# Graph layers on one core: re-timed hand-over between phases, and Z in f16 products from the twentieth tile on

## The chip, the cores and the metric

The kernel runs on 1 core of one Trainium2 chip. The metric is the device time of one execution in microseconds; lower is better. Three runs of the kernel before gave 885.96, 886.35 and 887.74, a median of 886.35 us.

## The reference, cut to what matters

```python
# x: 4096 x 256 f32, adj: 4096 x 4096 of zeros and ones
deg = max(adj.sum(-1), 1)
# layer 0: Z = x @ W0 is taken first, then the rows of adj are summed over Z
u  = adj @ (x @ W0) + x @ W0                    # pooled @ W, scaled by 1/deg
x1 = layernorm(x + relu(u / deg + x @ W0 + b0))
# layer 1
h = x1 @ Wsa;  sl = h @ a_left;  sr = h @ a_right
e = where(adj != 0, exp(-leaky_relu(sl[:, None] + sr[None, :], 0.01)), 0)
x_a = (e / (e.sum(1) + 1e-5)) @ h
x_b = adj @ (x1 @ Wg) + bg
attn_a, attn_b = sigmoid(adj @ (x1 @ wa) + x1 @ wa2 + ba), sigmoid(...)   # two gates per row
out = layernorm(x1 + sigmoid(attn_a * x_a + attn_b * x_b))
```

## The kernel before, in words

Rows are worked in tiles of 128 (T = 32), adj in strips of two row tiles by 512 columns (128 strips of 512 KB), cast to one byte ("codes") on ScalarE for even strips and on VectorE for odd ones (`cast`, L515 and L811). A ring of six strip buffers is filled by the SP queue: strip s is issued when strip s-6 is cast. Sixteen strips make one quarter (four row tiles), and the codes of each finished quarter are also written to DRAM by two DMAs of 1 MB (L324).

The order of the work on every engine is written out by hand, and engines wait on semaphores. Each engine takes its instructions in that order, so one that waits holds all behind it. The phases:

1. Z phase. For each tile t TensorE transposes x (`xt_step`, L1296), ScalarE copies it out of PSUM (`xt_copy`, L523), TensorE multiplies by W0 in f32 (`z_step`, L1307). Z is copied to SBUF by ScalarE for tiles below ZACT = 10 and by VectorE from there on (`z_copy`, L528 and L824). Z is split in two f16 parts, the high one on ScalarE (`y_hi`, L535), the low one on VectorE (`y_lo`, L851), once a scale is known that needs all of x. `split_at(t)` says how many splits stand in step t. From step 13 on TensorE adds one row block (8 matmuls, L1324) to the sums of the first four row tiles in each step. VectorE also prepares the weights of layer 1 in this phase (L858 to L875), once `load_weights` has brought them.
2. Row sums. 32 row tiles, 64 matmuls each (L1324). Two tiles behind, each tile is made into x1: VectorE `degree`, `residual`, `stats`; GpSimd the power -1/2 (L438) and a shift (L441); ScalarE `normalize` (L551); TensorE transposes x1 (`t_step`, L1344); ScalarE and VectorE split it (`x1t_copy` L560, `x1t_lo` L950); TensorE projects it by 12 matmuls (`p_step`, L1359); ScalarE `proj_copies` and VectorE `h_lo` and `forms_lo` store what layer 1 needs. The first projections stand between the quarters of tiles 4 and 5.
3. Ramp. The first products of layer 1 (`product`, L1417: seven products M1 to M7 of a Strassen step, for each pair of row tiles), the largest s over all rows (GpSimd L450), exponentials (L637), the mask on VectorE (`mask_chunk`, L1083), a high f16 part on ScalarE (`high_chunk`, L646), a low one on VectorE (`low_chunk`, L1090), and the matmuls with them (`e_chunk`, L1468, 48 matmuls).
4. Sixteen steps of layer 1 in a loop, with a tail for the last one.

In phase 3 the names below are E(s,c) for `e_chunk` of step s, chunk c; mask(s,c), high(s,c) and low(s,c) likewise.

Of the kernel before, what the change touches and what calls it, by code (L numbers as in the profile page):

```python
# [28 lines left out]
ZACT = 10  # L29
ZLAG = 12  # L30
OUTER = 16
LATE = 4
WTS = 13
WTS_AT = 8
# [54 lines left out]
def build(nc, x, adj, W0, b0, Wsa, asa, Wg, bg, Wa, ba, Wb, bb, out):  # L89
# [5 lines left out]
    class Area:  # L95
# [44 lines left out]
    wp = area("wp", [P, KD, WC], F32)  # L140
    xt = area("xt", [P, 2, D], F32)

# [36 lines left out]
    sc = area("sc", [P, 40], F32)  # L179
# [7 lines left out]
    col = iter(range(40))  # L187
# [6 lines left out]
    MH2 = column(2)  # L194

    BN, MV, VE, RS, SHIFT, DEG, REC = (
        slice(0, 6), slice(6, 8), slice(8, 9), slice(9, 10), slice(10, 11), slice(11, 12), slice(12, 13))
# [13 lines left out]
    with ExitStack() as ctx:  # L211
# [3 lines left out]
        for name in (  # L215
            "wts_in", "w0_in", "wsq_ready", "wsum_ready", "wnorm_ready", "alpha_pow",
            "const_ready", "xmax_part", "xmax_all", "wabs_ready", "wz_all", "sx_ready", "cast_act", "cast_dve",
            "xt_done", "xt_ready", "z_done", "zf_act", "zf_dve", "yhi_ready", "ylo_ready", "acc_done", "zb_ready",
            "r_ready", "stat_ready", "rstd_ready",
            "shift_ready", "x1_ready", "x1t_done", "x1t_ready", "x1t_lo_ready", "wps_ready", "proj_done",  # L220
            "g_ready", "gsum_ready", "ghi_ready", "forms_ready",
            "q_ready", "qa_ready", "hhi_ready", "hlo_ready", "nsr_ready",
            "nsr_max", "nmax_ready", "arg_ready", "rr_ready", "sl_ready", "slt_done", "slrow_ready", "sl_out",
# [184 lines left out]
        def _(pool):  # L408
# [26 lines left out]
            for n in range(T):  # L435
# [13 lines left out]
            pool.wait_ge(S["nsr_max"], 1)  # L449
            pool.partition_all_reduce(sc[:, NMAX], sc[:, NM], P, RMAX).then_inc(S["nmax_ready"], 1)  # L450
# [57 lines left out]
        def _(act):  # L508
# [9 lines left out]
            def xt_copy(t):  # L518
# [4 lines left out]
                act.copy(xt[:, t % 2, :], XTP(t)).then_inc(S["xt_ready"], 1)  # L523
# [13 lines left out]
            for t in range(T):  # L537
# [26 lines left out]
            def proj_copies(n):  # L564
# [39 lines left out]
            normalize(2)  # L604
            x1t_copy(1)
            normalize(3)
            proj_copies(1)
            x1t_copy(2)
            cast(2)
            proj_copies(2)  # L610
            x1t_copy(3)
            normalize(4)
            cast(2)
            for n in range(PT + 2, T + 3):
                proj_copies(n - 3)
                if n - 2 < T:
                    x1t_copy(n - 2)
                more = n // PT + 1 < NQ and n < T
                if more:
                    cast(1)  # L620
                if n - 1 < T:
                    normalize(n - 1)
                if more:
                    cast(1)
# [82 lines left out]
            def low_m67(u):  # L707

                gate(act, S["prod_done"], u * NPROD + NPROD, "passed_act")
# [39 lines left out]
            low_m67(0)  # L749
# [3 lines left out]
            low_m34(1)  # L753
# [33 lines left out]
            for e in range(2):  # L787
                act.wait_ge(S["attend_done"], NPAN + e)
                act.activation(sg[:, e, :], sg[:, e, :], ACT.Tanh, scale=sc[:, HINVA]).then_inc(S["sigmoid_ready"], 1)
                act.wait_ge(S["yshift_ready"], NPAN + e)  # L790
                if e == 0:
                    act.wait_ge(out_sent, 16 * (NPAN - 1))
                c, b = RS2.start + e, SH2.start + e
                act.activation(ot[:, e, :], sg[:, e, :], ACT.Identity, scale=sc1[:, c:c + 1], bias=sc1[:, b:b + 1]
                               ).then_inc(S["out_ready"], 1)
# [3 lines left out]
        def _(dve):  # L799
# [21 lines left out]
            def z_copy(t):  # L821

                dve.wait_ge(S["z_done"], t + 1)
                dve.tensor_copy(zf[:, t, 0:D], ZP(t)).then_inc(S["zf_dve"], 1)  # L824
# [9 lines left out]
            def z_scale():  # L834
# [9 lines left out]
                st.then(dve.tensor_scalar(sc[:, K64], sc[:, XG], 1.0 / EDGE_VAL, None, ALU.mult))  # L844
                dve.reciprocal(sc[:, SX], sc[:, XG]).then_inc(S["sx_ready"], 1)
# [724 lines left out]
```

## Time and profile before

| | |
|---|---|
| median of three runs | 886.35 us |
| profiled execution | 885.95 us, its span 884.1 us |
| TensorE busy | 857.5 us, 97% of the span |
| VectorE, ScalarE, GpSimd busy | 660.2, 588.4, 208.0 us |
| granted TensorE clock | 0.991 on average |
| DMA | 130.02 MB, mean 147 GB/s |

The profile is of one execution. Times in its timelines are microseconds from the start of the span, and a clock of 1.00 is full speed. An instruction's duration overlaps the next one's start by some hundredths, so prices are read from start to start.

### The profile page before, as it was taken

How to read it: one execution, taken by the hardware profiler on the slowest of the kernel's cores; microseconds unless marked ns; L12 is line 12 of the kernel's file. 1: busy time of each engine (PE TensorE's matmuls, PEld its weight loads, DVE VectorE, ACT ScalarE, POOL GpSimd, SP SyncE). 2: the span in 40 equal slices, each digit the busy share in tenths (PEclk: the TensorE clock that was granted, in tenths of full speed). 3: DMA queues.
4: the chain of work that ended last, by engine and by line, in shares of the span. 5: the costliest groups of instructions: out<-in, count | busy, mean ns of one | idle time of the engine just before them, and what ended most of it. 6: DMA issues, size and time to landing. Idle time of an engine off the chain costs nothing.

```text
span 884.1 us, 20483 instructions
## 1 busy us (share of the span) xinstructions
PE 857.5 (97%) x7573; PEld 756.1 (86%) x7573; DVE 660.2 (75%) x1146; ACT 588.4 (67%) x1246; POOL 208.0 (24%) x217
## 2 busy tenths in 40 slices
PE   7998899999999997999999999999999999999996
PEld 6887788888888885888888888888888888888886
DVE  5697465556465457898889988978978978978863
ACT  4664555655555436889877966967967867867832
POOL 1023244343433330110122022032032032032031
PEclk9999999999999999999999999999999999999999
DMA  9789999999989615101220220220220220220001
GB/s 323 226 318 328 340 352 349 382 299 347 364 299 362 217 55 193 54 8 49 79 79 1 77 77 9 68 77 0 77 77 0 77 77 0 77 77 0 25 24 37
DMA packets 67690, 130.02 MB, mean 147 GB/s; under 512 B 6544, under 2 KB 30128, under 8 KB 63152
## 3 DMA queue, kind: packets, MB, share of 16 engines
q1 hardware_dynamic: 58704, 120.87, 39.0%
q10 hardware_dynamic: 8928, 8.38, 2.9%
q8 instruction: 36, 0.59, 0.3%
q14 instruction: 22, 0.18, 0.1%
HBM read 99.87 MB, written 29.36 MB: 146 GB/s over the span
## 4 chain that ended last, share of the span: by engine, by line
PE 90%; DMA 3%; DVE 3%; ACT 1%; SPq 1%; issue 1%; POOL 1%; ACTq 0%; POOLq 0%; DVEq 0%
PE ps L1468 38%; PE ps L1324 22%; PE ps L1417 22%; PE ps L1359 5%; DMA strip<-in_adj_dram 2%; PE ps L1307 1%; DMA xs<-in_x_dram 1%; PE ps L1344 1%; SPq L330 0%; DVE sc L818 0%; PE ps L1296 0%; ACT codes L515 0%; SPq L312 0%; DVE ec L1083 0%; POOL fs L274 0%
## 5 line engine op out<-in xcount | busy, mean ns | idle before, releaser
L1468 PE MATMUL ps<-fb,em 128*128 128x257 f16 x3072 | 347.5, 273 | 0.0
L1468 PEld LDWEIGHTS ps<-fb,em 128*128 128x128 f16 x3072 | 300.5, 98 | 37.4
L1324 PE MATMUL ps<-y,codes 128*128 128x257 f16 x2048 | 238.7, 274 | 0.0
L1324 PEld LDWEIGHTS ps<-y,codes 128*128 128x128 fp8e4 x2048 | 200.9, 98 | 27.2 <-issue 0.3
L637 ACT ACTIVATE ec<-slb,nsb 128x256 f32<-128x256 f32 x512 | 210.8, 496 | 0.1
L1090 DVE SCALAR_TENSOR_TENSOR em<-ec,em 128x2048 f16<-128x2048 f32 x64 | 147.4, 2303 | 24.6 <-ACT em L646 24.6
L646 ACT ACTIVATE em<-ec 128x2048 f16<-128x2048 f32 x64 | 122.0, 1908 | 62.5 <-PE ps L1468 57.1
L1083 DVE SCALAR_TENSOR_TENSOR ec<-ec,pan 128x2048 f32<-128x2048 f32 x64 | 146.7, 2292 | 3.2 <-issue 1.8
L461 POOL TENSOR_TENSOR sc<-sc,sc 128x2 f32<-128x2 f32 x15 | 38.6, 2572 | 245.2 <-DVE sc L1178 245.2
L1417 PE MATMUL ps<-zz,dd 128*128 128x256 f16 x768 | 89.4, 273 | 1.4 <-DVE t L1112 1.4
L1417 PEld LDWEIGHTS ps<-zz,dd 128*128 128x128 fp8e4 x768 | 75.1, 98 | 10.4 <-DVE t L1112 1.7
L515 ACT ACTIVATE codes<-strip 128x1024 uint8<-128x1024 f32 x64 | 66.8, 1048 | 8.6 <-DMA strip<-in_adj_dram 7.0
L455 POOL TENSOR_TENSOR w<-w,bgb 128x512 f32<-128x512 f32 x16 | 27.9, 1744 | 175.8 <-DVE w L1140 156.9
L1417 PE MATMUL ps<-fa,pan 128*128 128x260 f16 x512 | 62.6, 282 | 5.2 <-DVE s L1120 3.9
L944 DVE SCALAR_TENSOR_TENSOR dd<-pan 128x512 uint32<-128x512 uint32 (+2 forms) x85 | 64.2, 815 | 0.0
L551 ACT ACTIVATE x<-x,lnst 128x256 f32<-128x256 f32 x32 | 19.2, 600 | 67.4 <-POOL lnst L441 67.4
L1417 PEld LDWEIGHTS ps<-fa,pan 128*128 128x128 fp8e4 x512 | 51.3, 100 | 13.7 <-issue 4.2
L1417 PE MATMUL ps<-fa,dd 128*128 128x260 f16 x512 | 59.5, 274 | 0.4 <-DVE m L1102 0.4
L438 POOL TENSOR_TENSOR lnst<-lnst,sc 128x1 f32<-128x1 f32 x32 | 27.2, 850 | 137.5 <-DVE lnst L988 134.7
L960 DVE TENSOR_SCALAR lnst<-ps 128x1 f32<-128x1 f32 x32 | 5.0, 157 | 72.2 <-PE ps L1324 72.2
L1417 PEld LDWEIGHTS ps<-fa,dd 128*128 128x128 fp8e4 x512 | 49.9, 98 | 7.3 <-issue 0.6
L1359 PE MATMUL ps<-wps,x1t 128*128 128x256 f16 (+1 forms) x384 | 48.6, 277 | 6.8 <-DVE x1t L950 6.8
(149 smaller groups left out, 808.8 us busy)
## 6 DMA issues: line engine op xcount, KB each, us to landing
strip<-in_adj_dram SPq DMA_DIRECT2D x128, 512.0 KB, 7.1
a_scratch<-codes SPq DMA_DIRECT2D x16, 1024.0 KB, 9.7
pan<-a_scratch SPq DMA_DIRECT2D x16, 1024.0 KB, 5.1
x_scratch<-x ACTq DMA_DIRECT2D x32, 128.0 KB, 5.2
x1r<-x_scratch SPq DMA_DIRECT2D x16, 256.0 KB, 2.8
h_scratch<-hst ACTq DMA_DIRECT2D x30, 136.0 KB, 5.5
out_dram<-ot SPq DMA_DIRECT2D x15, 256.0 KB, 2.2
fb<-h_scratch SPq DMA_DIRECT2D x3, 1088.0 KB, 8.7
```

The source lines that it names most:

```text
L455: pool.tensor_tensor(w[:], w[:], bgb[:].unsqueeze(1).broadcast_to([P, 2, D]), ALU.add).then_inc(S["bias_ready"], 1)
L461: pool.tensor_tensor(sc1[:, RS2], sc1[:, VE2], sc[:, MH2], ALU.pow).then_inc(S["yrstd_ready"], 1)
L515: act.activation(codes_of(s), strip_of(s), ACT.Copy, scale=float(EDGE - NONE), bias=float(NONE)).then_inc(S["cast_act"], 1)
L637: e_ = act.activation(ec[:, c % ER, jj, :], slb[:, slot, :], ACT.Exp, scale=-(1 - SLOPE), bias=nsb[:, jb:jb + 1])
L646: act.activation(em[:, c, 0], ec[:, c % ER], ACT.Copy, scale=MU / EDGE_VAL).then_inc(S["ehigh_ready"], 1)
L944: return dve.scalar_tensor_tensor(out=o, in0=b, scalar=0x7f7f7f7f, in1=a, op0=ALU.bitwise_and, op1=ALU.bitwise_xor)
L1083: dve.scalar_tensor_tensor(out=ec[:, c % ER], in0=ec[:, c % ER], scalar=1.0, in1=pan[:, slot, c * CH:(c + 1) * CH, :].bitcast(F8), op0=ALU ...
L1090: dve.scalar_tensor_tensor(out=em[:, c, 1], in0=ec[:, c % ER], scalar=MU / EDGE_VAL, in1=em[:, c, 0], op0=ALU.mult, op1=ALU.subtract).then ...
L1324: mm = pe.matmul(ACC(n), codes[:, qq % SLOTS, h, jb, e * P:(e + 1) * P].bitcast(F8), y[:, jb, part, 0:YC], start=(jb == 0 and part == 0), ...
L1359: mm = pe.matmul(b, x1t[:, n % 2, x_part, k * P:(k + 1) * P], wps[:, k, w_part, c0:c1], start=(k == 0 and x_part + w_part == 0), stop=(k = ...
L1417: mm = pe.matmul(ps[:, bank, 0:2 * c], a.bitcast(F8), g, start=(p == 0), stop=(p == NP - 1))
L1468: mm = pe.matmul(PH(2 * m + e)[:, 0:HC], em[:, c, e_part, i, e * P:(e + 1) * P], fb[:, jb, h_part, 0:HC], start=(jb == 0 and e_part + h_pa ...
```

## The change

- Z phase. ScalarE copies Z for two more tiles (ZACT 12) and casts a first strip before it waits for the scale. Two of three steps hold a cast on each engine, where it was one of two: 27 strips are cast in the phase, where it was 21. Layer 1's weights are issued after strip 6, where it was after 8, and their preparation on VectorE stands four steps later. The splits come three in two steps.
- Z from tile 20 on. x and W0 are scaled and split in two f16 parts; Z is three products for each half of K, six f16 matmuls where there were two in f32. ScalarE writes the high part of x's transpose, VectorE the low one (`xt_lo`), and the product is scaled back in `z_copy`. W0's parts (`w0_parts`) stand on VectorE between the copy of tile 12 and the first `y_lo`.
- `normalize` is one instruction on VectorE (subtract, multiply) where it was a shift on GpSimd and an instruction on ScalarE. The same in the tail for the last two tiles, not in the loop.
- Between tiles 3 and 6 fewer casts stand ahead of `proj_copies`; `forms_hi` is a step of its own, behind `x1t_copy`.
- Ramp. The maximum over partitions is a TensorE transpose and a VectorE reduction, not GpSimd's all-reduce. The exponentials start ahead of the copies `low_m34` and `low_m1`. M3 and M4 of the second pair are moved ahead of and behind M7 of the first one. On VectorE low(0,0) is ahead of mask(0,1), and the row factors come after it.

```diff
-ZACT = 10
+ZACT = 12
+ZF16 = 20
-WTS_AT = 8
+WTS_AT = 6
-            upto = lambda i: 0 if i < ZACT else min(i - 1, 2 * (i - ZACT) + 2)
+            upto = lambda i: 0 if i < ZACT else min(i - 1, 3 * (i - ZACT) // 2 + 2)
@@ ScalarE, Z phase
+                    act.activation(xth[:, t % 2, 0, :], XTP(t), ACT.Copy, scale=sc[:, XK]
+                                   ).then_inc(S["xt_ready"], 1)
-                if t >= 11 and t % 2 == 1:
+                if t == ZACT - 1 or t > ZACT and t % 3 != 0:
                     cast(1)
@@ VectorE, Z phase
             for t in range(ZACT, T):
+                if ZF16 <= t + 1 < T:
+                    xt_lo(t + 1)
                 z_copy(t)
+                if t == ZACT:
+                    w0_parts()
                 for i in split_at(t):
                     y_lo(i)
-                if t >= 12 and t % 2 == 0:
+                if t % 3 != 1:
                     cast(1)
@@ TensorE, Z phase
+                if t >= ZF16:
+                    pe.wait_ge(S["xt_lo_ready"], t - ZF16 + 1)
+                    for x_part, w_part in ((0, 0), (0, 1), (1, 0)):
+                        mm = pe.matmul(ZP(t), xth[:, t % 2, x_part, k * P:(k + 1) * P], w0s[:, k, w_part, :], ...)
@@ VectorE, row sums
+            def normalize(n):
+                ln = lnst[:, n % 2, :]
+                dve.wait_ge(S["rstd_ready"], n + 1)
+                dve.tensor_scalar(x1[:, n % X1RING, :], x1[:, n % X1RING, :], ln[:, 6:7], ln[:, RS], ALU.subtract,
+                                  ALU.mult).then_inc(S["x1_ready"], 1)
@@ ScalarE, tiles 3 to 6
-            normalize(0)
-            cast(3)
+            cast(1)
             x1t_copy(0)
-            normalize(1)
-            cast(2)
+            cast(1)
             proj_copies(0)
@@ ScalarE, ramp
-            low_m34(0)
-            low_m1(0)
             act.wait_ge(S["slb_ready"], 2)
-            exp_chunk(0, 0, 0, first=True)
-            exp_chunk(0, 0, 1, first=True, behind={6: lambda u: low_m52(u, first=True)})
+            exp_chunk(0, 0, 0, first=True, behind={4: low_m34, 5: low_m1, 7: lambda u: low_m52(u, first=True)})
+            exp_chunk(0, 0, 1, first=True, behind={6: lambda u: low_m67(u, first=True)})
             high_chunk(0, 0, True)
-            low_m67(0)
+            act.wait_ge(S["m52_read"], 1)
+            low_m34(1)
             act.wait_ge(S["arg_ready"], 1)
             act.activation(rr[:], tb[:], ACT.Exp).then_inc(S["rr_ready"], 1)
             high_chunk(0, 1, True)
-            low_m34(1)
             exp_chunk(0, 0, 2, first=True)
@@ VectorE, ramp
             middle(0)
             middle_m1(0)
-            row_factors()
-            dve.wait_ge(panel_in[1], 16)
             some_differences(1, 1, DIFF_ORDER[0:2], done=4)
             mask_chunk(0, 0, 0)
+            read_67(0)
+            row_ends()
+            read_52(0, first=True)
-            sums_52(0, first=True)
+            low_chunk(0, 0)
+            add_52(0, first=True)
+            add_67(0)
+            some_differences(1, 1, DIFF_ORDER[2:], done=NPROD + 1)
             mask_chunk(0, 0, 1)
-            sums_67(0)
-            low_chunk(0, 0)
-            some_differences(1, 1, DIFF_ORDER[2:])
+            row_factors()
             middle(1)
             low_chunk(0, 1)
@@ TensorE, ramp
+            pe.wait_ge(S["mid_read"], 1)
+            pe.wait_ge(panel_in[1], 16)
+            product(1, "M3")
             pe.wait_ge(S["mid_read"], 2)
             product(0, "M7")
+            product(1, "M4")
```

## Rows read from the trace of the kernel before

**Rows 1.** The page: busy time of TensorE, and GB/s in 40 equal slices.
```profile
PE 857.5 (97%) x7573; PEld 756.1 (86%) x7573; DVE 660.2 (75%) x1146; ACT 588.4 (67%) x1246; POOL 208.0 (24%) x217
...
GB/s 323 226 318 328 340 352 349 382 299 347 364 299 362 217 55 193 54 8 49 79 79 1 77 77 9 68 77 0 77 77 0 77 77 0 77 77 0 25 24 37
```

**Rows 2.** Waits of TensorE: us in total, times, longest.
```profile
PE ps L1359 <- DVE x1t L950: 6.8, 3, 3.5
```

**Rows 3.** Timeline of TensorE, Z phase: start, duration, what, count, idle before.
```profile
21.57 1.62 PE L1307 MATMUL ps<-w,xt 128*128 128x256 f32 x4 [2.96 <-ACT xt L523]
...
25.45 1.07 PE L1324 MATMUL ps<-y,codes 128*128 128x257 f16 x8
...
26.58 1.03 PE L1307 MATMUL ps<-w,xt 128*128 128x256 f32 x4
27.44 1.04 PE L1324 MATMUL ps<-y,codes 128*128 128x257 f16 x8
28.32 0.38 PE L1296 MATMUL ps<-ident,xs 128*128 128x128 f32 x2
...
61.70 14.24 PE L1324 MATMUL ps<-y,codes 128*128 128x257 f16 x128
```

**Rows 4.** Timeline of VectorE, Z phase.
```profile
48.32 1.23 DVE L866 TENSOR_TENSOR wsq<-wp 128x1036 f32<-128x1036 f32 x1
...
50.20 0.42 DVE L824 COPY zf<-ps 128x256 f32<-128x256 f32 x1
50.53 2.40 DVE L851 SCALAR_TENSOR_TENSOR y<-zf,sc,y 128x256 f16<-128x256 f32 x1
...
59.04 0.48 DVE L851 SCALAR_TENSOR_TENSOR y<-zf,sc,y 128x256 f16<-128x256 f32 x1
59.43 0.69 DVE L811 TENSOR_SCALAR codes<-strip 128x1024 uint8<-128x1024 f32 x1
60.03 0.42 DVE L824 COPY zf<-ps 128x256 f32<-128x256 f32 x1
```

**Rows 5.** Busy us by stretch: PE, PEld, DVE, ACT, POOL; clock; DMA share; GB/s.
```profile
24.00:28.00 4.00, 4.00 (x24) 3.12 (x24) 2.61 (x8) 3.53 (x8) 0.00 (x0) 0.81 0.48 137
...
350.00:354.00 4.00, 3.03 (x15) 2.12 (x16) 3.77 (x8) 3.07 (x6) 0.00 (x0) 0.50 0.02 4
```

**Rows 6.** Timelines of ScalarE and TensorE, tile 4.
```profile
82.83 1.06 ACT L515 ACTIVATE codes<-strip 128x1024 uint8<-128x1024 f32 x1 [3.54 <-DMA strip<-in_adj_dram]
...
86.52 2.41 PE L1359 MATMUL ps<-wps,x1t 128*128 128x262 f16 x12 [3.53 <-DVE x1t L950]
88.72 2.72 PE L1324 MATMUL ps<-y,codes 128*128 128x257 f16 x16
```

**Rows 7.** Timelines of ScalarE, VectorE and TensorE, ramp.
```profile
340.59 0.51 ACT L594 ACTIVATE zz<-fs 128x384 f16<-128x384 f32 x1
...
357.81 3.30 ACT L637 ACTIVATE ec<-slb,nsb 128x256 f32<-128x256 f32 x8
...
364.37 1.22 ACT L654 ACTIVATE sc<-sc,rab,sc 128x1 f32<-128x1 f32 x4
...
366.94 3.69 ACT L646 ACTIVATE em<-ec 128x2048 f16<-128x2048 f32 x2
...
347.99 2.28 DVE L1083 SCALAR_TENSOR_TENSOR ec<-ec,pan 128x2048 f32<-128x2048 f32 x1
...
357.07 1.89 DVE L944 SCALAR_TENSOR_TENSOR dd<-pan 128x512 uint32<-128x512 uint32 x3
...
371.18 0.28 DVE L1110 TENSOR_TENSOR t<-lc,t 128x128 f32<-128x128 f32 x1
...
350.97 6.43 PE L1417 MATMUL ps<-fa,pan 128*128 128x260 f16 x32 [3.94 <-DVE s L1120]
...
374.84 1.91 PE L1417 MATMUL ps<-zz,dd 128*128 128x256 f16 x16
```

**Rows 8.** Timeline of GpSimd, tail.
```profile
881.07 0.26 POOL L481 TENSOR_SCALAR sc<-sc 128x1 f32<-128x1 f32 x1
```

More of the change, by code:

```diff
@@ L194, in build @@
     MH2 = column(2)
-    BN, MV, VE, RS, SHIFT, DEG, REC = (
-        slice(0, 6), slice(6, 8), slice(8, 9), slice(9, 10), slice(10, 11), slice(11, 12), slice(12, 13))
+    XA, WA, XK, WK, IZ = (column() for _ in range(5))
+    BN, MV, VE, RS, DEG, REC = (
+        slice(0, 6), slice(6, 8), slice(8, 9), slice(9, 10), slice(10, 11), slice(11, 12))
     small = iter(range(48))
@@ L823, in z_copy, with xt_lo @@
                 dve.wait_ge(S["z_done"], t + 1)
-                dve.tensor_copy(zf[:, t, 0:D], ZP(t)).then_inc(S["zf_dve"], 1)
+                if t < ZF16:
+                    dve.tensor_copy(zf[:, t, 0:D], ZP(t)).then_inc(S["zf_dve"], 1)
+                else:
+                    dve.tensor_scalar(zf[:, t, 0:D], ZP(t), sc[:, IZ], None, ALU.mult).then_inc(S["zf_dve"], 1)
+            def xt_lo(t):
+                dve.wait_ge(S["xt_ready"], t + 1)
+                dve.scalar_tensor_tensor(out=xth[:, t % 2, 1, :], in0=XTP(t), scalar=sc[:, XK], in1=xth[:, t % 2, 0, :],
+                                         op0=ALU.mult, op1=ALU.subtract).then_inc(S["xt_lo_ready"], 1)
             def z_bound():
@@ L999, in _ @@
             cast(1)
+            normalize(0)
             head(1)
             x1t_lo(0)
-            cast(2)
+            normalize(1)
+            cast(1)
             head(2)
-            cast(2)
+            h_lo(0)
+            normalize(2)
+            x1t_lo(1)
+            cast(1)
             head(3)
-            h_lo(0)
-            x1t_lo(1)
-            cast(3)
             h_lo(1)
+            x1t_lo(2)
+            normalize(3)
             forms_lo(0)
-            x1t_lo(2)
+            cast(1)
             h_lo(2)
             x1t_lo(3)
+            cast(2)
             head(4)
-            cast(2)
+            h_lo(3)
+            normalize(4)
+            cast(1)
             for n in range(PT + 2, T + 3):
@@ L1036, in _ @@
                 if more:
-                    cast(2)
+                    cast(1)
+                if n - 1 < T:
+                    normalize(n - 1)
+                if more:
+                    cast(1)
                 if T - 2 <= n <= T:
@@ L1054, in _, with row_ends @@
             dve.tensor_scalar(slb[:], slb[:], sc[:, NMAX], None, ALU.min).then_inc(S["slb_ready"], 1)
+            forms_lo(NP - 1)
+            for op in DIFF_ORDER:
+                difference(0, op, NP - 2, NP).then_inc(S["diff_ready"], 1)
+            def row_ends():
+                h_lo(T - 1)
+                dve.wait_ge(S["slt_done"], 1)
+                dve.tensor_scalar(slrow[:], ps[0:T, 5, 0:P], sc[0:T, NMAX], None, ALU.min
+                                  ).then_inc(S["slrow_ready"], 1)
             def row_factors():
-                h_lo(T - 1)
                 for c in range(2):
@@ L1123, in sums_52, with add_52 @@
                 s_.then_inc(S["m52_read"], 1)
+            def add_52(u, first=False):
+                wq = w[:].rearrange("p e (h c) -> p (e h) c", c=P)
                 if not first:
```

146 lines of the change are left out of this document (81 added, 65 removed).

## The prediction, made before the changed kernel was run

> **What bounds the kernel now.** I read the busy shares first: TensorE is busy 97% of the span [rows 1], so the time is its work plus its gaps. The long loop of layer 1 shows no wait of TensorE, and the diff leaves it alone. The waits of TensorE and its timelines then give three places with gaps: 2.96 us in the Z phase [rows 3], 6.8 us in three waits of `p_step` around tiles 4 to 6 [rows 2], of which one is 3.53 us [rows 6], and 3.94 us in the ramp [rows 7]. After a long gap the matmuls are slow: 32 take from 350.97 to 357.24 or 0.196 us each [rows 7], against 0.110 us normally (8 from 27.44 to 28.32 [rows 3]); the granted clock was 0.50 in 350 to 354 [rows 5], the lower level of 1.2 GHz. So a long gap costs itself and up to 2.7 us more. The timelines of ScalarE and VectorE at these places decide what the new orders give.
>
> **Term A, the Z phase.** TensorE's step was 0.25 (transposes) + 0.86 (z in f32) + 0.88 (row block) = 1.98 us [rows 3]. Six f16 matmuls at 0.110 are 0.66, so 12 tiles save 12 x 0.20 = 2.4 us of TensorE.
>
> The start. ScalarE waits for the scale two steps later, so two z steps are done ahead of it. VectorE knows the scale later (three to five small dependent operations, 0.2 to 1.2 us; I take 0.6) and then does `w0_parts`: two operations of 512 elements, nearest row the squares with 1036 and 518 elements in 1.88 us [rows 4], so 0.7 to 1.9, taken as 1.2. The first row block, at 25.45 before, then starts at about 23.0 (22.3 to 24.4). Z of tile 19 ends at 23.0 + 0.88 + 6 x 1.98 + 1.11 = 36.9.
>
> The rest. TensorE alone would need 0.88 + 8 x 1.79 + 3 x 0.91 + 0.66 = 18.6 us and be through at 55.5; before it was at 61.70 [rows 3]. But VectorE must write xt_lo(31) before z(31). From the copy of tile 19 to there it has 11 copies of 0.33, 16 `y_lo` of 0.39, 7 casts of 0.60, the squares of 1.88 [rows 4], 11 `xt_lo`, four weight columns, and 1.9 us in which GpSimd's reduction holds one of its operations (2.40 us for a `y_lo` that takes 0.48 elsewhere [rows 4]). `xt_lo` is not in the trace; a copy from PSUM (0.33) and a `y_lo` (0.39) bound it, I take 0.36. A weight column is a 256-element operation and a read, 0.45. Sum: 3.6 + 6.2 + 4.2 + 1.9 + 4.0 + 1.8 + 1.9 = 23.6 us. With 1.3 us in which it still waits for TensorE and ScalarE in steps 20 to 22, that ends at 61.8; z(31) and its latency make 62.6. So from about step 23 VectorE sets the pace, and the f16 products buy nothing.
>
> The DMA stands beside it. By then 27 strips (14.2 MB), x and W0 (4.3), the weights (1.0) and the codes of quarter 0 (2.1) must have moved, 21.6 MB; at 352 GB/s [rows 1] from 2 us on that is 63.4. Before, the ring ran dry at times (137 GB/s in 24 to 28 [rows 5]) because casts came late. I take the end of the phase at 63.0, so A = +1.3. Its ends are -6.2 (VectorE hides all) and +8 (rival below). TensorE's gaps near steps 28 and 29 come out at 2 to 3 us each, near the length after which its clock fell.
>
> The Trainium skill, page GPSIMD Engine Reference, section Specifications, says that GpSimd's SBUF interface clashes with VectorE operations that have two SBUF inputs. `y_lo` has two, `xt_lo` reads PSUM and one SBUF tile; the 2.40 us row agrees. By that rule the hold falls on a `y_lo` behind xt_lo(28), and TensorE's gap of some 4 us there is split in two; without it A would be 1 to 2 us more.
>
> **Term B, tiles 4 to 6.** The cause of the 3.53 us is visible on ScalarE: it sat in a cast for a strip that had not landed (3.54 us, ending at 82.83 [rows 6]), with `proj_copies(0)` behind it. Now strips up to 26 are cast by tile 4, one cast instead of two or three stands ahead of each copy, and `normalize` no longer waits for GpSimd on ScalarE. I followed the new orders: `p_step(1)` is wanted at 82.8 and its x1t_lo is there at 82.2; `p_step(3)` at 93.0 and 92.8; x1 of tile 4 at 97.9 and 97.9. All hold, two by nothing. What comes back is 6.8 us of waits [rows 2] and the slow clock behind 86.52: 12 matmuls in 2.20 for 1.32 and 16 in 2.56 for 1.76 [rows 6], 1.7 us. B = -8.4; if the tight ones slip by 1 to 3 us each, -4.
>
> VectorE's new instruction there is 0.4 us a tile (by the 0.33 to 0.39 above) in an 8.6 us tile; it waits for GpSimd's power in VectorE's order, with one cast ahead of it. Queued behind it are the next cast and `degree`, neither due at once. ScalarE loses 0.6 us a tile. Beyond tile 6 TensorE has no gap, so that buys nothing.
>
> **Term C, the ramp.** The maximum by a transpose and a reduction (together about 0.6 us, both small) frees ScalarE's exponentials at once after its copies, at about 341.0 [rows 7]. 16 exponentials of 0.41 (3.30 for 8), four copies of 0.25 to 0.3, then high(0,0) of 1.85 end at 350.6. TensorE starts M3 of the second pair earlier, and E(0,0) starts at 352.9, 8 us earlier than before. That gain does not last. On ScalarE the exponential of the row factors waits for `row_factors`, and high(0,1) and everything else is queued behind it. VectorE gets there late: low(0,0) 2.2 from 350.6, sums 1.3, three differences 1.8, mask(0,1) 2.2 (2.28 with its overlap), row factors 1.1: 359.2 [rows 7]. ScalarE idles from 350.9 to 359.2. From there: high(0,1) 2.0 to 361.2, 16 exponentials 6.6 to 367.9 with `low_m1`, gates and gated 2.57 (364.37 to 366.94) to 370.5, high(0,2) 1.85 to 372.3; VectorE low(0,2) 2.2 and `middle_m1` 0.55 to 375.1. M7 of the second pair, at 374.84 before, can't start before 375.2. TensorE has done E(0,1) by 368.8, so it idles 6.4 us and resumes at the low clock: 1.7 to 2.7 us, taken as 2.1. The new early bias add on GpSimd runs beside VectorE's mask, +0.7 (a hold as above; 0 to 1.5). C = 0.3 + 2.1 + 0.7 = +3.1. Its ends are -8 (ScalarE's queue is not held) and +5. Later steps have VectorE some 3 us behind the old order and TensorE as much, so nothing more is lost.
>
> **Term D, the tail.** The shift (0.26 [rows 8]) and its hand-over go, and VectorE's instruction is shorter than ScalarE's: -0.6.
>
> **Sum.** 885.95 (profiled execution: 884.1 of span and 1.85 around it) + 1.3 - 8.4 + 3.1 - 0.6 = 881.35. The median of the runs shown is 0.4 us above that execution, within their spread, so I forecast 881.3.
>
> **Rivals.**
> 1. The Z phase gains as well: VectorE keeps up (the hold is small, `xt_lo` is hidden) and A is -6.2: 881.3 - 7.5 = 873.8. For it: casts and splits fit TensorE's pace in every step without weights (0.33 + 0.36 + 0.59 + 0.40 = 1.68 against 1.79). Against it: the weights fall into just these steps.
> 2. The ramp gains: C is about -6 and the time 872.2. For it: TensorE's order is free of waits to E(0,0). Against it: the ScalarE queue as worked out.
> 3. The tile 4 to 6 waits move to other places (two are tight by 0.2 us) and B is -3: 886.7, no difference.
> 4. Slower: the Z phase becomes bound by DMA. Place: casts of strips 22 to 26 on ScalarE in steps 28 to 31, ahead of the transposes' copies. At 318 GB/s, the slowest later slice [rows 1], 21.6 MB need 68 us and the phase ends at 70.6; TensorE starts the sums at the low clock. A = +8.9 + 2: 890.9. It decides from about 332 GB/s downwards (phase end 67.8, with the low clock behind it). For it: slices of 318 and 328 beside a busy ring. Against it: those slices held gaps in which nothing was asked for [rows 5].
>
> **Chances.** Forecast 0.50 (its own range 877 to 885), rival 1 0.20, rival 2 0.10, rival 3 0.08, rival 4 0.12. Range 873 to 886: rivals 2 and 4 are outside, 0.2 in all. A measurement of this kernel can tell 0.2% (1.8 us) from no change. Faster by more than that: 0.50 + 0.20 + 0.10 = 0.80; within: 0.08; slower: 0.12.
>
> **What would show it.** A: VectorE without idle time from about 46 us on, an operation of about 2.4 us behind the squares, z matmuls waiting for VectorE's xt, and the long row-sum run at about 63. Right if TensorE's f16 z step is 0.66 us. B: no wait of `p_step` on x1t_lo over 1 us. C: ScalarE idle for 8 us before the exponential of the row factors, TensorE idle for about 6 us before M7 of the second pair, and a low clock in the E(0,2) behind it. The prediction is wrong if the sums begin before 60, if M7 starts with no gap, or if any wait appears in the loop.

## The result, and the profile after

The changed kernel takes 893.07 us (median of four runs, 892.39 to 894.1), the kernel before 886.15 us beside it: a ratio of 1.008 with a 95% interval of 1.0062 to 1.0098. It is slower by some 7 us; the forecast was 881.3 us, a gain of 4.7 us on the profiled execution, and the time lies above the range of 873 to 886. Its profiled execution took 892.42 us with a span of 890.2 us and a mean clock of 0.988.

The page's first section and slices, for [rows 1]:

```profile
PE 857.3 (96%) x7598; PEld 754.8 (85%) x7598; DVE 691.7 (78%) x1198; ACT 571.8 (64%) x1214; POOL 183.8 (21%) x182
...
GB/s 320 304 358 194 335 386 314 380 311 333 371 299 343 227 65 181 53 3 54 78 54 26 77 77 0 77 77 0 77 77 0 77 77 0 77 77 0 25 25 36
```

TensorE's busy time is the same, VectorE has 31.5 us more. The waits of TensorE (total, times, longest), for [rows 2]:

```profile
PE ps L1377 <- DVE xth L821: 8.7, 8, 3.5
PE ps L1487 <- DVE t L1152: 4.8, 1, 4.8
PE ps L1373 <- ACT xt L521: 3.7, 3, 3.1
```

The wait of `p_step` on x1t_lo is gone from the list. In its place stand waits in the Z phase (L1377 is the f16 product, L1373 the f32 one) and in the ramp (L1487, `product`).

TensorE's timeline in the Z phase, for [rows 3]:

```profile
23.26 1.05 PE L1394 MATMUL ps<-y,codes 128*128 128x257 f16 x8 [2.17 <-DVE y L863]
...
37.44 1.13 PE L1373 MATMUL ps<-w,xt 128*128 128x256 f32 x4 [3.09 <-ACT xt L521]
...
60.60 0.82 PE L1377 MATMUL ps<-w0s,xth 128*128 128x256 f16 x6 [2.09 <-DVE xth L821]
61.26 0.38 PE L1357 MATMUL ps<-ident,xs 128*128 128x128 f32 x2
65.15 1.44 PE L1377 MATMUL ps<-w0s,xth 128*128 128x256 f16 x6 [3.51 <-DVE xth L821]
...
70.85 15.32 PE L1394 MATMUL ps<-y,codes 128*128 128x257 f16 x128
86.01 0.38 PE L1414 MATMUL ps<-ident,x 128*128 128x128 f32 x2
```

The first row block starts 2.2 us earlier than before. The 128 matmuls that end the phase start 9.15 us later, and take 15.32 us where they took 14.24. The two long gaps have one cause, which ScalarE's timeline shows in its last column (the 3.09 us ahead of 37.44 and the 3.51 us ahead of 65.15): a cast (L512) waits for a strip that has not landed, and the copy of x's transpose (L521, in f16 L525) is queued behind it.

```profile
36.07 1.06 ACT L512 ACTIVATE codes<-strip 128x1024 uint8<-128x1024 f32 x1 [4.79 <-DMA strip<-in_adj_dram]
37.04 0.35 ACT L521 COPY xt<-ps 128x256 f32<-128x256 f32 x1
...
63.06 1.06 ACT L512 ACTIVATE codes<-strip 128x1024 uint8<-128x1024 f32 x1 [5.00 <-DMA strip<-in_adj_dram]
64.03 0.46 ACT L525 ACTIVATE xth<-ps,sc 128x256 f16<-128x256 f32 x1
```

SP's queue says why the strips are late (start, time to issue, what):

```profile
20.08 0.98 SPq L313 DMA_DIRECT2D wp<-in_L_gnn_W_gcnb_dram  x2
...
27.24 1.34 SPq L323 DMA_DIRECT2D sc<-in_L_gnn_bb_dram  x1
28.63 22.95 SPq L342 DMA_DIRECT2D strip<-in_adj_dram  x15
51.70 0.88 SPq L330 DMA_DIRECT2D a_scratch<-codes  x2
52.61 19.54 SPq L342 DMA_DIRECT2D strip<-in_adj_dram  x11
```

The twelve small DMAs of layer 1's weights keep the queue from 20.08 to 28.58, and strips 7 and on stand behind them. The buffer for strip 7 came free at 24.2, when strip 1 was cast, so of these 8.5 us the last 4.4 held a strip back. The two writes of codes (2.1 MB) go out at 51.70, ahead of strip 22, which the cast at 63.06 waits for. Stretches of the same execution (columns as in [rows 5]):

```profile
28.00:32.00 4.00, 4.00 (x31) 3.44 (x29) 3.31 (x8) 2.79 (x6) 0.00 (x0) 1.00 0.38 98
...
56.00:60.00 4.00, 2.51 (x23) 2.08 (x21) 3.97 (x8) 1.48 (x4) 0.00 (x0) 1.00 1.00 406
60.00:64.00 4.00, 1.03 (x8) 0.76 (x8) 3.32 (x5) 0.94 (x1) 3.84 (x1) 0.85 1.04 403
64.00:68.00 4.00, 2.03 (x9) 1.30 (x10) 2.46 (x7) 3.13 (x8) 0.01 (x1) 0.50 1.04 387
```

At 28 to 32 the DMA moved 98 GB/s, and from 56 to 68 it was full (share 1.00 to 1.04, 387 to 406 GB/s). Over the whole phase, 2 to 70.85, its share was 0.96 at a mean of 334 GB/s. The clock fell to 0.50, its 1.2 GHz level, after the gaps.

The ramp on ScalarE, VectorE and TensorE, for [rows 7]:

```profile
362.49 0.23 ACT L747 ACTIVATE rr<-tb 128x32 f32<-128x32 f32 x1 [9.72 <-DVE tb L1112]
```

```profile
356.24 2.96 DVE L960 SCALAR_TENSOR_TENSOR dd<-pan 128x512 uint32<-128x512 uint32 x3
359.13 2.28 DVE L1123 SCALAR_TENSOR_TENSOR ec<-ec,pan 128x2048 f32<-128x2048 f32 x1
```

```profile
355.31 5.44 PE L1546 MATMUL ps<-fb,em 128*128 128x257 f16 x48 [0.42 <-DVE em L1130]
...
378.54 3.57 PE L1487 MATMUL ps<-zz,dd 128*128 128x256 f16 x16 [4.77 <-DVE t L1152]
381.91 16.86 PE L1546 MATMUL ps<-fb,em 128*128 128x257 f16 x144
398.61 3.60 PE L1487 MATMUL ps<-fa,pan 128*128 128x260 f16 x31
```

ScalarE idles 9.72 us ahead of the exponential of the row factors, TensorE 4.77 us ahead of M7 of the second pair, and both blocks behind it run slowly at first (3.57 us for 1.91, 16.86 for 16.00). The tail, for [rows 8]:

```profile
887.63 0.41 DVE L1265 TENSOR_SCALAR ot<-sg,sc 128x256 f32<-128x256 f32 x1 [0.68 <-POOL sc L479]
```

**Where the 6.1 us of span went**, from landmarks of both timelines. The transposes of tile 0 behind the 128-block moved from 75.78 to 86.01: A = +10.2. Those of tile 6 moved from 123.91 to 125.73: B = -8.4. The next common landmark in layer 1, the product behind the 144 matmuls that begin with E(0,2), moved from 392.43 to 398.61, with +1.8 carried into the ramp: C = +4.4. One wait in the loop grew from 0.36 to 0.79 (at 450.62), +0.4. The last 192 matmuls of TensorE moved from 856.02 to 862.63, and from there to the end it is 27.57 us for 28.08: D = -0.5. The sum is +6.1, as 890.2 - 884.1.

### The profile page after: what moved, and what is told of

It reads as the page before. It is cut to its first block, busy times and chain, and to the rows that moved or that the text cites. A ratio compares the mean times of both kernels' runs of the same rounds, so it can differ in the third digit from the quotient of the medians.

```text
span 890.2 us, 20515 instructions
## 1 busy us (share of the span) xinstructions
PE 857.3 (96%) x7598; PEld 754.8 (85%) x7598; DVE 691.7 (78%) x1198; ACT 571.8 (64%) x1214; POOL 183.8 (21%) x182
## 4 chain that ended last, share of the span: by engine, by line
PE 74%; issue 8%; DVE 7%; ACT 5%; POOL 2%; DMA 1%; SPq 1%; POOLq 0%; ACTq 0%; DVEq 0%
PE ps L1546 29%; PE ps L1394 21%; PE ps L1487 18%; PE ps L1429 4%; ACT ec L634 3%; ACT em L643 1%; DVE ec L1123 1%; PE ps L1373 1%; DVE dd L960 1%; DVE em L1130 1%; DMA strip<-in_adj_dram 1%; PE ps L1414 1%; POOL zb L437 0%; POOL wsum L426 0%; PE ps L1348 0%
## 5 line engine op out<-in xcount | busy, mean ns | idle before, releaser
L1487 PE MATMUL ps<-zz,dd 128*128 128x256 f16 x768 | 91.1, 276 | 4.9 <-DVE t L1152 4.8
L1487 PEld LDWEIGHTS ps<-zz,dd 128*128 128x128 fp8e4 x768 | 75.8, 99 | 14.8 <-issue 5.4
L512 ACT ACTIVATE codes<-strip 128x1024 uint8<-128x1024 f32 x64 | 65.5, 1048 | 17.4 <-DMA strip<-in_adj_dram 16.2
L455 POOL TENSOR_TENSOR w<-w,bgb 128x512 f32<-128x512 f32 x16 | 26.1, 1634 | 192.8 <-DVE w L1190 192.8
L1487 PE MATMUL ps<-fa,dd 128*128 128x260 f16 x512 | 61.3, 279 | 3.2 <-DVE m L1142 3.2
L1487 PE MATMUL ps<-fa,pan 128*128 128x260 f16 x512 | 60.0, 274 | 1.4 <-DVE zz L946 1.1
L1487 PEld LDWEIGHTS ps<-fa,dd 128*128 128x128 fp8e4 x512 | 50.7, 99 | 11.2 <-issue 3.7
L557 ACT ACTIVATE x1t<-ps 128x256 f16<-128x256 f32 x32 | 12.3, 384 | 74.5 <-PE ps L1414 74.5
L1487 PEld LDWEIGHTS ps<-fa,pan 128*128 128x128 fp8e4 x512 | 49.9, 98 | 8.5 <-DVE zz L946 1.4
L444 POOL TENSOR_TENSOR lnst<-lnst,sc 128x1 f32<-128x1 f32 x32 | 25.3, 789 | 151.2 <-DVE lnst L1004 151.2
L800 DVE TENSOR_SCALAR codes<-strip 128x1024 uint8<-128x1024 f32 x64 | 50.2, 786 | 1.9 <-DMA strip<-in_adj_dram 1.8
L572 ACT ACTIVATE q<-ps,sc 128x1 f32<-128x1 f32 x32 | 11.2, 351 | 61.2 <-PE ps L1429 61.2
```

What stands on the lines that cost most here:

```text
L512: act.activation(codes_of(s), strip_of(s), ACT.Copy, scale=float(EDGE - NONE), bias=float(NONE)).then_inc(S["cast_act"], 1)
L800: dve.tensor_scalar(codes_of(s), strip_of(s), float(EDGE - NONE), float(NONE), ALU.mult, ALU.add).then_inc(S["cast_dve"], 1)
L1487: mm = pe.matmul(ps[:, bank, 0:2 * c], a.bitcast(F8), g, start=(p == 0), stop=(p == NP - 1))
```

## The experiments

Twelve kernels ran, on three chips. Each ratio is to the kernel before on the same chip, with its 95% interval. A span and its landmarks are of one execution, and these differ: the kernel before took 882.92 to 887.4 us in 23 runs on one chip.

**1. The weights one strip earlier** (`wts5`).

```diff
-WTS_AT = 6
+WTS_AT = 5
```

> The changed kernel with one number different: layer 1's weights are issued after strip 5, not after strip 6. Theory S (the strips set the Z phase): the twelve small issues held the SP queue for 8.5 us while strips 7 and 8 were wanted, and ScalarE then waited 4.8 us for strip 8; after strip 5 the queue has nothing to do until strip 0 is cast, so the 3.1 us gap of TensorE near 35 us goes, the row sums start at 67 to 68 instead of 70.85, and the time is 889.5 to 890.5. Rival V (VectorE sets the pace of the phase): the gap comes back as waits for VectorE's low parts, the row sums start at 70 or later, and the time stays at 892.5 to 893.5.

Measured: 892.91 us, ratio 1.0089 (1.0069 to 1.011), span 890.0. That is the rival's time: the wait near 37 went and nothing was gained. TensorE's timeline:

```profile
37.48 1.13 PE L1373 MATMUL ps<-w,xt 128*128 128x256 f32 x4 [0.32 <-ACT xt L521]
...
71.00 15.02 PE L1394 MATMUL ps<-y,codes 128*128 128x257 f16 x128
```

So the first of the two gaps sets nothing: the second stands as before, where a cast still waited 4.19 us, and the row sums start at the same time. Two later runs say the same without any edit in this phase: in `rampexp` and `rampold` TensorE's gap near 37 was 0.34 and 0.20 us, and the row sums started at 71.48 and 71.33. So this gap comes and goes from one execution to the next, and that it went here isn't shown to be the edit's doing. The twelve small DMAs now took 12.7 us to issue (15.25 to 27.94) behind x and six strips, so strip 7 went out hardly earlier than before. The first row block started at 24.39, 1.1 us later, but it did so in `rampexp` and `rampold` too (24.15, 24.42).

**2. Z in f32 throughout** (`zf32`).

```diff
-ZF16 = 20
+ZF16 = 32
```

> The changed kernel with Z in f32 for all tiles: the f16 products, their split of x on VectorE (12 operations of 0.4 us) and the scaled copy don't occur; the two operations for W0's parts remain. Theory S (strips set the phase): TensorE's six waits for VectorE's low part go but the two long waits of ScalarE for strips stay, the row sums start at 69 to 71 and the time is 891.5 to 893. Rival V (VectorE sets the pace): 4.8 us of its work goes and TensorE gains 2.4 us of work it has room for, the row sums start at 66 to 67, and the time is 888.5 to 889.5. If the f16 products pay, the time rises to 895.

Measured: 891.48 us, ratio 1.0074 (1.0053 to 1.0095), span 888.3.

```profile
64.22 2.07 PE L1373 MATMUL ps<-w,xt 128*128 128x256 f32 x4 [4.59 <-ACT xt L521]
...
69.86 14.25 PE L1394 MATMUL ps<-y,codes 128*128 128x257 f16 x128
```

With 12 `xt_lo` less on VectorE (`w0_parts`, 1.2 us, still ran) the strip's gap stands in one piece, and the row sums start 1 us earlier, at the full clock, so the 128-block ends 2.1 us earlier (83.95). That is theory S: with the strips held, VectorE's extra work decides little.

**3. The exponentials ahead of the row factors** (`rampexp`). On ScalarE the exponentials of chunk 2 and 3 and high(0,1) no longer stand behind the wait for `row_factors`.

```diff
             low_m34(1)
-            act.wait_ge(S["arg_ready"], 1)
-            act.activation(rr[:], tb[:], ACT.Exp).then_inc(S["rr_ready"], 1)
-            high_chunk(0, 1, True)
-
             exp_chunk(0, 0, 2, first=True)
...
             exp_chunk(0, 0, 3, first=True)
+            high_chunk(0, 1, True)
+            act.wait_ge(S["arg_ready"], 1)
+            act.activation(rr[:], tb[:], ACT.Exp).then_inc(S["rr_ready"], 1)
             gates(0, 0)
```

> The changed kernel with ScalarE's order in the ramp different: exponentials of chunks 2 and 3 stand ahead of high(0,1), and the exponential of the row factors behind it. Theory Q (ScalarE's queue held 9.7 us by one wait decides the ramp): M7 of the second pair starts about 6 us earlier (372.5 instead of 378.5), its gap shrinks from 4.8 to about 2 us, E(0,2) starts at about 374.5 instead of 381.9, and the time is 885 to 887. Rival (VectorE's own work decides the ramp): M7 starts at most 1.5 us earlier and the time is 891.5 or more.

Measured: 888.27 us, ratio 1.0035 (1.0021 to 1.0049), span 884.9, 5.3 us below the changed kernel's. By the two ratios, 1.0035 and 1.0080, it is 4 us. TensorE's waits:

```profile
372.89 1.91 PE L1486 MATMUL ps<-zz,dd 128*128 128x256 f16 x16 [1.12 <-DVE t L1151]
...
409.13 3.71 PE L1486 MATMUL ps<-fa,dd 128*128 128x260 f16 x32 [0.89 <-DVE m L1141]
426.49 3.71 PE L1486 MATMUL ps<-fa,pan 128*128 128x260 f16 x32 [1.34 <-DVE s L1160]
```

The place is the one that the prediction named: the 4.77 us gap falls to 1.12, E(0,2) starts 7.3 us earlier, at 374.64, and runs at the full clock, so that the landmark of 398.61 comes 8.1 us earlier, at 390.48. Of that, 2.6 us come back as waits for VectorE in the loop's first steps (0.89, 1.34 and, at 445.37, 1.13, where the changed kernel has 0.79).

**4. The ramp's orders as before** (`rampold`): the three engines' orders of the ramp from the kernel before, the maximum by transpose and reduction kept.

```diff
+            low_m34(0)
+            low_m1(0)
             act.wait_ge(S["slb_ready"], 2)
-            exp_chunk(0, 0, 0, first=True, behind={4: low_m34, 5: low_m1, 7: lambda u: low_m52(u, first=True)})
+            exp_chunk(0, 0, 0, first=True)
...
```

> The changed kernel with the ramp's order on all three engines as before the change (the maximum over partitions stays a transpose and a reduction). By my reading of the trace the new ramp costs 4.4 us between the end of the row sums and E(0,2), so the time is 888.2 to 889.2, and a little less since the exponentials still start earlier. Rival: the loop behind takes up what the ramp loses, and the time stays within 1 us of 893.

Measured: 887.28 us, ratio 1.0018 (1.0005 to 1.003), span 884.2. From the end of the row sums to the last block it is 526.55 us (330.06 to 856.61), with 532.62 in the changed kernel and 527.83 before. So the new orders cost 6.1 us in these two executions. The 1.3 us below the kernel before are not the new maximum's gain: behind the same 3.94 us gap the 32 slow matmuls took 5.11 us here and 6.27 before, and 5.20 to 6.03 in the later kernels with the new maximum, so 1.2 us of it is how long the clock stayed low.

**5. The codes writes ten strips later** (`codeslate`).

```diff
-                if s >= RING and (s - RING) % GS == GS - 1:
-                    codes_when_cast((s - RING) // GS)
+                if s >= GS and s % GS == GS - 1:
+                    codes_when_cast(s // GS - 1)
```

> The changed kernel with the two writes of each quarter's codes to DRAM (2.1 MB) issued ten strips later, so that strips 22 to 31 are ahead of the first pair in the queue. Theory S (strips set the end of the Z phase): strip 22 lands at about 57 instead of 63, ScalarE's wait of 5.0 us ahead of the copy for z(29) goes, the row sums start at 65 to 67 instead of 70.85 and at full clock, and the time is 887 to 889. Rival V (VectorE sets the pace): the row sums start at 69 or later, 891.5 or more.

Measured: 890.24 us, ratio 1.0055 (1.0036 to 1.0075), span 888.8.

```profile
62.28 0.81 PE L1377 MATMUL ps<-w0s,xth 128*128 128x256 f16 x6 [2.15 <-DVE xth L821]
...
65.53 1.44 PE L1377 MATMUL ps<-w0s,xth 128*128 128x256 f16 x6 [2.12 <-DVE xth L821]
...
70.09 14.24 PE L1394 MATMUL ps<-y,codes 128*128 128x257 f16 x128
```

The wait for strip 22 fell from 5.00 to 0.24 us, so the writes ahead of it were its cause. But TensorE now waits for VectorE, and the block starts 0.8 us earlier only and, at the full clock, ends 1.8 us earlier (84.17). The place is rival V's, the time lies between the two forecasts. Two limits stood at nearly the same height: strips at 70.85, VectorE at 70.09, this one with the first gap still in it (3.71 us).

**6. The same on the kernel before** (`b4_codeslate`), the diff of 5.

> The kernel before with the same one move (writes of the codes ten strips later). If the 3.5 us wait of ScalarE for a strip at 82.8 came from these writes ahead of strips 22 to 31, the wait and the slow clock behind it go: 5 us less, 880 to 882 against 885.6. If it came from the late casts and the ring alone, it stays within 1 us of 885.6.

Measured: 893.33 us, ratio 1.0085 (1.0062 to 1.0109), span 892.5. TensorE's timeline around tiles 4 to 6:

```profile
87.50 2.06 PE L1359 MATMUL ps<-wps,x1t 128*128 128x262 f16 x12 [3.52 <-DVE x1t L950]
...
101.11 2.77 PE L1359 MATMUL ps<-wps,x1t 128*128 128x262 f16 x12 [6.71 <-DVE x1t L950]
```

Neither branch had this. The 3.53 us wait, which the expectation wanted to explain by the writes, stayed (3.52), though its strip, number 30, now went out ahead of them: it came from the late casts and the ring. And the write that no longer stood among the Z phase's strips stood ahead of those for tiles 4 to 6 (issued at 80.17), and TensorE waited 6.71 us there where it had waited 1.33.

**7. What seemed best of both, with f32** (`mix_f32`): the edits of 4, 5 and 2, and no `w0_parts`.

```diff
-                if t == ZACT:
+                if t == ZACT and ZF16 < T:
```

> The changed kernel with the ramp's order as before, the codes' writes ten strips later, and Z in f32 throughout without W0's parts. Theory S: the Z phase is free of long waits for strips and of VectorE's extra work, the row sums start at 62 to 64 instead of 70.85, tiles 4 to 6 keep their 8.4 us, and the time is 877 to 880. If the Z phase has yet another bound that I have not seen, the row sums start after 66 and the time is 882 or more.

Measured: 886.2 us, ratio 1.0011 (0.9996 to 1.0027), span 882.6: no difference from the kernel before, and 6 us above the forecast: its second branch, a further bound. The cast at 36.34 still waited 5.35 us for a strip, and the row sums began at 66.58 and at the low clock, so that the block ended at 81.75. Strips and f16 taken away together give 4.3 us at this landmark (86.0), `w0_parts` included; alone they gave 1.8 and 2.1.

**8. Casts re-spaced as well** (`mix_late`).

```diff
-WTS_AT = 6
+WTS_AT = 8
@@ ScalarE, VectorE: Z phase
-                if t == ZACT - 1 or t > ZACT and t % 3 != 0:
+                if t >= ZACT - 1 and t % 2 == 1:
-                if t % 3 != 1:
+                if t % 2 == 0:
@@ ScalarE: behind the Z phase
-            cast(1)
+            cast(4)
             x1t_copy(0)
@@ VectorE: behind the Z phase
+            cast(1)
             head(0)
-            cast(1)
+            cast(2)
             normalize(0)
             head(1)
+            cast(1)
```

> As mix_f32, but with the casts in one of two steps of the Z phase as before the change, the weights after strip 8, and the six casts that are left in the stretch in which ScalarE and VectorE wait for the first row sums. Theory: demand for strips in the Z phase falls by six strips, 3.1 MB or 8 us of DMA, so the phase runs at TensorE's pace: row sums at 59 to 60.5, and if the six casts are hidden behind the row sums, the time is 875 to 877. If they delay tiles 4 to 6 instead, part of the 8.4 us is lost again and the time is 879 to 883.

Measured: 878.99 us, ratio 0.9926 (0.9907 to 0.9945), span 877.7. This version beats both kernels.

```profile
59.92 14.25 PE L1394 MATMUL ps<-y,codes 128*128 128x257 f16 x128
...
92.13 1.50 PE L1429 MATMUL ps<-wps,x1t 128*128 128x262 f16 x12 [2.93 <-DVE x1t L968]
```

The row sums start 6.7 us earlier than in `mix_f32`, as expected, and the waits around tiles 4 to 6 are 5.5 us (1.08, 1.49, 2.93), where `mix_f32` has 2.4.

**9. Only the casts re-spaced** (`cadence`): the diff of 8 on the changed kernel, nothing else.

> The changed kernel with only the casts re-spaced: one step in two holds a cast on each engine in the Z phase, as before the change (21 strips), layer 1's weights are issued after strip 8, and the six casts taken out stand behind the Z phase. The f16 products, the ramp and everything else are as in the changed kernel. Theory S (the faster casts ran into strips that had not landed, and in-order ScalarE and VectorE passed that wait on to TensorE): no cast in the Z phase waits over 1 us for a strip, the row sums begin at 61.5 to 63.5 instead of 70.85 at the full clock, and some 3 to 6 us of waits come back around tiles 4 to 6; span 885 to 887. Rival F (the f16 products' work on VectorE costs the time, whatever the strips do): row sums not before 66, span 889 or more.

Measured: 887.68 us, ratio 1.0021 (1.0009 to 1.0033), span 887.6.

```profile
58.34 1.05 PE L1379 MATMUL ps<-w0s,xth 128*128 128x256 f16 x6 [2.04 <-DVE xth L821]
...
65.64 14.24 PE L1396 MATMUL ps<-y,codes 128*128 128x257 f16 x128
80.69 0.44 PE L1416 MATMUL ps<-ident,x 128*128 128x128 f32 x2 [0.81 <-DVE x L1010]
```

No cast waits over 0.40 us for a strip in the phase, and TensorE is through with the block at 79.9 for 86.0. The edit takes back 6.1 us of A. It moves the casts and the weights together, and which of the two does it was not run apart. The start of 65.64 lies between the two forecasts: the remaining gaps are waits for VectorE. The profiled execution, 889.8 us, was the slowest of ten, so its span overstates the time: by the ratios (1.0021 for 1.0080) this kernel is 5.2 us faster than the changed one, by the spans 2.6.

**10. The same with the ramp's old orders** (`mix_early_f16`): 9 and 4 together.

> As cadence, but with the orders of the ramp as before the change. The ramp was worth 6.0 us of span when it alone was undone (890.2 to 884.2). Theory: terms add, since the loop has no waits: span 879 to 881, 6 us below cadence. Rival: the later terms absorb part of an earlier gain, difference under 4 us.

Measured: 882.32 us, ratio 0.9961 (0.995 to 0.9973), span 879.8. That is 5.4 us below 9 by the medians and 7.8 by the spans. At the transposes of tile 4 its profile is already 1.8 us ahead (104.13 for 105.90), which nothing in its edits explains; 9 is read from the slowest of its ten executions. In 4 the ramp's old orders gave 5.5 us by the ratios and 6.0 by the spans, so the terms add.

**11. The same with Z in f32** (`mix_early`): `ZF16 = 32` and the diff of 7.

> As mix_early_f16, but Z in f32 throughout and no parts of W0. Against mix_early_f16 this is the price of the f16 products where strips do not hold: theory V (VectorE sets the pace there, so TensorE's 2.4 us are not collected and xt_lo and w0_parts are extra work on the engine that decides): row sums 1 to 3 us earlier than with f16, span 877 to 879. Rival: the f16 products pay once strips are out of the way, and this one is 1 to 2 us slower than mix_early_f16. Against mix_late it has the codes writes at their old place, six strips behind, where mix_late has them ten strips later: waits around tiles 4 to 6 fall from 5.5 us to 3 to 5, at the price of a strip wait near 60.

Measured: 880.16 us, ratio 0.994 (0.992 to 0.9959), span 877.5. TensorE in 11, and VectorE first in 10 and then in 11:

```profile
22.24 1.05 PE L1394 MATMUL ps<-y,codes 128*128 128x257 f16 x8 [1.23 <-DVE y L865]
...
60.77 15.16 PE L1394 MATMUL ps<-y,codes 128*128 128x257 f16 x128
76.58 0.44 PE L1414 MATMUL ps<-ident,x 128*128 128x128 f32 x2 [0.66 <-DVE x L1012]
```

```profile
57.53 0.48 DVE L823 SCALAR_TENSOR_TENSOR xth<-ps,sc,xth 128x256 f16<-128x256 f32 x1
57.92 0.48 DVE L818 TENSOR_SCALAR zf<-ps,sc 128x256 f32<-128x256 f32 x1
58.31 1.94 DVE L865 SCALAR_TENSOR_TENSOR y<-zf,sc,y 128x256 f16<-128x256 f32 x1
```

```profile
54.13 0.42 DVE L816 COPY zf<-ps 128x256 f32<-128x256 f32 x1
54.47 2.40 DVE L865 SCALAR_TENSOR_TENSOR y<-zf,sc,y 128x256 f16<-128x256 f32 x1
```

In f16 each step of VectorE holds one instruction more, and TensorE's product waits for it; in f32 the product waits for nothing that VectorE does in the same step. VectorE reaches the held `y_lo` 3.8 us earlier without f16 (54.47 for 58.31). TensorE is through with the 128-block at 75.9 (76.58 less its wait), where 10 had 79.97. So the f16 products, which save TensorE 2.4 us, cost 4.1 us of the phase where strips don't hold (with `w0_parts`, which went too). Up to 1.0 of it may be the two executions: x's last part was there 1.0 us later in 10 (17.82 for 16.84, the start of its reduction on VectorE). The start moved by 4.7 us, more than the 1 to 3 expected. Of the whole time the f16 products cost less, 2.2 us by the medians, with intervals that just overlap, since more waits stand around tiles 4 to 6 without them (3.1 us for 1.5). Against `mix_late`, the strip wait came (3.00 us, at 67.09, behind the phase) and the waits around tiles 4 to 6 fell to 3.1 us, as expected, for the same span.

**12. The codes writes five strips later** (`mix_mid`), on 8.

```diff
-                if s >= GS and s % GS == GS - 1:
-                    codes_when_cast(s // GS - 1)
+                if s >= 11 and (s - 11) % GS == GS - 1:
+                    codes_when_cast((s - 11) // GS)
```

> As mix_late, but the codes writes five strips earlier (issued behind strip 26 in place of 31; the old place is 21). Theory: the two 1 MB writes then fall into the stretch behind the last cast of the Z phase, 56 to 64, where the queue moved only 72 GB/s in 56 to 60, so strips for tiles 4 to 6 land up to 5 us earlier: waits around tiles 4 to 6 2 to 4 us instead of 5.5, row sums unchanged at 59.9, span 875 to 877. Rival: the order of the writes moves the waits without lowering their sum, span 877 to 879.

Measured: 881.09 us, ratio 0.9943 (0.9926 to 0.996), span 877.9. The waits around tiles 4 to 6 sum to 4.2 us (2.27, 0.33, 0.27 and, at 113.81, 1.30) for 5.5 and 3.1, and the time is no better than with either other place: spans 877.5, 877.7 and 877.9, and intervals that overlap. That is the rival: the order moves the waits and barely lowers their sum. Once the casts are spaced right, the place of the writes is worth nothing that can be measured.

## Why the prediction was wrong

**Term A, forecast +1.3, measured +10.2: the failed step.** The step was "at 352 GB/s [rows 1] from 2 us on that is 63.4 ... I take the end of the phase at 63.0". It treated the strips as a volume over a mean rate. As a volume it was short by 2.8 us: the 21.6 MB had moved at 66.2, a mean of 337 GB/s for 352, and the stretch at 28 to 32, behind the weights' DMAs, alone held back 1.0 MB. What it had no term for is the order. With 2.1 MB of codes ahead of it strip 22 was there at 63.0, ScalarE stood still for 5.00 us on it, and the copies for the last three tiles, the f16 products that need them and the low clock came behind: 7.8 us more. Casting six strips fewer in the phase, with the weights later, takes back 6.1 of the 10.2 us (`cadence`).

Rival 4 had the place (casts of strips 22 and on holding ScalarE), the size (A = +10.9) and the time (890.9), with a chance of 0.12. That its sum came so near is in part luck: its 318 GB/s did not occur (334 over the phase), and it counts nothing of the f16 products' 2.1 to 4.1 us. The prediction's range was also narrower than its chances: rival 3, at 886.7, lies outside it too, 0.30 in all where it says 0.2.

The second half of the step failed too, more quietly. VectorE's account ended at 62.6 with 27 casts; the row sums started at 70.09 with strips held only once (`codeslate`, 3.71 us), and with 21 casts at 65.5. Of the 3 us and more that it was short, sizes give 1.2: `xt_lo` 0.40 for 0.36 and the scaled copy 0.39 for 0.33, twelve of each. The rest is that f16 puts a VectorE instruction into TensorE's chain of every step, so the engines wait for each other in turn; that this is all of the rest I have not shown.

Right in A were the first row block (23.26, forecast 23.0), the f16 step (0.66 us: 60.60 to 61.26), `w0_parts` (1.18 us for 1.2), the low clock behind the last gaps, and the hold: the `y_lo` behind the squares took 1.95 us (start 60.77) for 0.48. The hold cost some 0.4 us less than forecast, since `xt_lo` and the copy of z run ahead of the `y_lo` now: GpSimd's reduction began at 60.16 and the instruction behind the `y_lo` started at 62.64, 2.48 us later, and before the change it was 50.37 and 52.85, 2.48 us too. The gap split in two, as forecast, stands by itself where no strip is late (2.04 and 1.18 us in `cadence`). The Trainium skill, page GPSIMD Engine Reference, section Specifications, names the clash for VectorE operations with two SBUF inputs. The traces agree: the copy of z, which reads PSUM, takes its usual 0.39 us beside the reduction (60.38 to 60.77), and the `y_lo` behind it is held. The `xt_lo` has only 0.2 us beside it, too little to tell.

What A is made of, by landmark at the end of the 128-block (before 75.8, after 86.0): casts spaced as before, 79.9; and f32 besides, 75.9. In the other order f32 alone gives 83.95, and the casts (with `w0_parts` gone) then 8.0. The f16 products cost 2.1 us where strips hold and, with `w0_parts`, 4.1 where they don't.

**Term B, forecast -8.4, measured -8.4.** The waits of `p_step` on x1t_lo are gone, the two tight ones with them. But it was not all a gain of the new orders. With 21 strips cast in the Z phase, the rest as in the changed kernel, B is -4.9 in `cadence` and -6.7 in `mix_early_f16`: the new orders give that much by themselves, and the six more strips bought the other 1.7 to 3.5 us and cost 6.1 in A. The prediction priced the two sides of this trade as independent terms.

**Term C, forecast +3.1, measured +4.4 and +0.4 in the loop.** The mechanism is the one forecast: ScalarE idle for 9.72 us (8.3) behind the wait for the row factors, TensorE idle and slow behind it. The sizes were off by little. M7 of the second pair started 1.9 us later than before, with what was carried in taken off, for 0.3 + 0.7: the differences beside GpSimd's bias add took 2.96 us for 1.89, +1.1 for the +0.7 allowed, and the row factors came behind them. The low clock behind M7's gap cost 2.5 us for 2.1. Of "it idles 6.4 us", 4.77 us stand ahead of M7 and 2.37 us already ahead of the 32 matmuls at 363.12. "Nothing more is lost" in later steps was wrong by the 0.4. `rampexp` and `rampold` show that this term was avoidable.

**Term D, forecast -0.6, measured -0.5.** The final layer norm is one instruction with a hand-over of 0.68 us.

## What to carry over

A queue of transfers is to be costed in its order, transfer by transfer, with what stands ahead of each one that an engine waits for; a mean rate hides an issue stall or a write in between, and an in-order engine passes the wait on to everyone. Where two limits stand close together, the price of one is not seen from its wait: taking away a wait of 5.0 us gave 1.8 us here, f32 alone 2.1, a spacing of the casts that eased both 6.1, and with f32 10.1. Work saved on the busiest engine by adding a step on the second busiest can be a loss, as it was here, where that step comes into the chain of each tile. And a profile is one execution: the one of `cadence` was 2.1 us above its median, nearly as much as the difference that was to be read from it.

## What the runs showed of the hardware

- Twelve small DMAs cost SP's queue 6.0 us to issue in the kernel before (28.45 to 34.41), 8.5 us in the changed one, and 12.7 us directly behind x and six strips of 512 KB (`wts5`). The Trainium skill, page DMA: Bandwidth & Descriptors, section Rules for kernel authors, says that spreading DMAs over issuing engines brings no bandwidth and only saves issue time. Here the issue time held strip 7 back by 4.4 us, and no run shows that this moved the end of the phase. Issuing the weights from another engine was not tried.
- Three differences on VectorE took 2.96 us beside a GpSimd operation of 1.55 us that began within them (at 356.51), 1.89 us without it.
- A `y_lo` beside GpSimd's reduction is held until 2.48 us after the reduction's start, whether it begins 0.16 us behind that start (2.40 us long, before) or 0.61 us (1.95 us long, after); `codeslate`, `cadence`, `mix_early_f16` and `mix_early` give the same 2.48.
- After TensorE gaps of 2.09 and 3.51 us (58.5 to 60.6 and 61.6 to 65.15) the clock stood at 0.50 through the next stretch, and six f16 products took 1.2 us start to start (65.15 to 66.38) for 0.66.
